# Blocks of 3, 2 and 3 matmul pairs, transposed maxima evicted by ScalarE in the first gap, and maxima 12 steps ahead

## The reference

```
for c in range(6):                      # 6 nodes, each on 4 sequences
    q = ew[c,0] * (nodes[in_q] @ We[eq] + be[eq])    # k and v alike
    scores = (q @ Wq[c]) . (k @ Wk[c]) / sqrt(16)    # 8 heads, 1024 x 1024
    attn = softmax(scores)
    nodes[c] = act_w[c] * (attn @ (v @ Wv[c])) @ Wo[c] + q
out = layernorm(nodes[5])
```

## Time and profile before

| | |
|---|---|
| median of 3 runs | 2479.15 us (2472.24 to 2482.92) |
| profiled execution: its time | 2468.93 us |
| its span in the trace | 2467.0 us |
| PE busy | 2297.7 us, 93% |
| DVE busy | 2062.4 us, 84% |
| ACT busy | 1787.8 us, 72% |
| POOL busy | 466.2 us, 19% |

### The profile page before, as it was taken

One profiled execution on the slowest core, in us unless ns is written; L12 is line 12 of the kernel. 1 busy time (PEld: TensorE's weight loads), 2 busy tenths in 40 slices (PEclk: granted clock), 3 DMA queues, 4 the chain that ended last, 5 costly groups with the idle time before them and its releaser, 6 DMA issues.

```text
span 2467.0 us, 40455 instructions
## 1 busy us (share of the span) xinstructions
PE 2297.7 (93%) x15067; PEld 929.7 (38%) x15067; DVE 2062.4 (84%) x2319; ACT 1787.8 (72%) x3425; POOL 466.2 (19%) x594
## 2 busy tenths in 40 slices
PE   6588899999999999999999999999999999999996
PEld 3433333333333333333433333333433333433332
DVE  6477778888888888888889888888888888889883
ACT  3225566777777777778777777778778778787775
POOL 1311121121121121121121121121121122123201
PEclk8568998999999999999999999999999999999998
DMA  3311131341342332332332242242232242242201
GB/s 95 79 31 32 27 60 40 63 83 46 73 76 50 71 73 53 68 73 54 68 73 55 66 75 51 52 76 50 51 77 49 52 77 53 47 86 58 60 16 49
DMA packets 75938, 147.43 MB, mean 60 GB/s; under 512 B 21451, under 2 KB 39135, under 8 KB 75743
## 3 DMA queue, kind: packets, MB, share of 16 engines
q0 software_dynamic: 28800, 96.49, 21.1%
q1 hardware_dynamic: 46942, 48.36, 7.3%
HBM read 40.40 MB, written 13.34 MB: 22 GB/s over the span
## 4 chain that ended last, share of the span: by engine, by line
PE 78%; DVE 13%; ACT 5%; issue 2%; POOL 1%; DMA 1%; SPq 0%; POOLq 0%; ACTq 0%; DVEq 0%
PE ring L431 29%; PE context L483 28%; DVE max_neg L979 8%; PE wide L453 7%; ACT e_ring L730 5%; PE ring L381 2%; PE ring L401 2%; PE ring L373 2%; PE ring L392 2%; PE ring L406 2%; DVE max_part L983 1%; PE ring L304 1%; PE ring L462 1%; PE ring L305 1%; DVE mixing L778 1%
## 5 line engine op out<-in xcount | busy, mean ns | idle before, releaser
L979 DVE TENSOR_REDUCE max_neg<-wide 128x1 f32<-128x1024 f32 x1536 | 1825.8, 1219 | 301.6 <-PE wide L453 289.4
L730 ACT ACTIVATE e_ring<-ring 128x512 f32<-128x512 f32 x3072 | 1628.6, 603 | 438.8 <-PE ring L431 437.2
L453 PE MATMUL wide<-k_aug,q_aug 48*128 48x512 f32 x3072 | 1128.2, 454 | 67.6 <-DVE max_neg L979 52.7
L431 PE MATMUL ring<-q_aug,k_aug 50*128 50x512 f32 x3072 | 1095.2, 446 | 4.8 <-ACT e_ring L730 3.1
L483 PE MATMUL context<-e_ring,v_aug 128*32 128x512 f32 (+1 forms) x7696 | 870.7, 525 | 0.1
L431 PEld LDWEIGHTS ring<-q_aug,k_aug 50*128 50x128 f32 x3072 | 502.3, 186 | 814.7 <-ACT e_ring L730 510.6
L453 PEld LDWEIGHTS wide<-k_aug,q_aug 48*128 48x128 f32 x3072 | 499.1, 188 | 152.2 <-DVE max_neg L979 117.2
L483 PEld LDWEIGHTS context<-e_ring,v_aug 128*32 128x32 f32 x7696 | 152.0, 108 | 280.7 <-issue 224.3
L263 POOL DMA_DIRECT2D src<-node_dram x40 | 23.7, 593 | 719.8 <-PE ring L392 719.8
L1056 POOL CAST q_part<-q_part 128x512 fp32r<-128x512 f32 x48 | 29.4, 612 | 445.2 <-ACT q_part L659 444.9
L1056 POOL CAST k_part<-k_part 128x512 fp32r<-128x512 f32 x48 | 29.3, 611 | 341.3 <-ACT k_part L651 341.2
(11 more groups left out here) (230 smaller groups left out, 876.4 us busy)
## 6 DMA issues: line engine op xcount, KB each, us to landing
k_aug<-k_part POOLq DMA_DIRECT2D x144, 256.0 KB, 7.1
q_aug<-q_part POOLq DMA_DIRECT2D x144, 256.0 KB, 7.3
src<-node_dram POOLq DMA_DIRECT2D x40, 512.0 KB, 5.5
ctxT<-raw SPq DMA_DIRECT2D x384, 32.0 KB, 2.0
rden_bc<-rden_dram SPq DMA_DIRECT2D x23, 512.0 KB
node_dram<-node_ring SPq DMA_DIRECT2D x16, 512.0 KB, 2.9
q_aug<-max_rows SPq DMA_DIRECT2D x384, 4.0 KB
node_ring<-in_L_attn_x SPq DMA_DIRECT2D x4, 512.0 KB, 5.1
```

What stands on the lines that cost most here:

```text
L431: e.matmul(bk[:, :], k_aug[first:first + AUG, u % 2, h // 2, chunk * P:(chunk + 1) * P].bitcast(F32R), q_aug[first:first + AUG, u % 2, h / ...
L453: done = e.matmul(wide[w % 2][:, half_of(kh)], q_aug[first:first + SPLIT, u % 2, h // 2, q0:q0 + P].bitcast(F32R), k_aug[first:first + SPL ...
L730: e.activation(e_ring[:, n % E_SLOTS, :], bank[where["st", n]][:, :], ACT.Exp, scale=EXP_SCALE).then_inc(a_exp, 1)
L979: e.tensor_reduce(max_neg[:, G % 2, row:row + 1], wide[w % 2][:, :], AX_X, ALU.max, negate=True).then_inc(v_mx, 1)
```

## The change

- The blocks are 3, 2 and 3 pairs: pairs 0, 1, 2, first gap, pairs 3, 4, second gap, pairs 5, 6, 7, third gap. What the second gap holds (a half of `weighted`, or the product) stays. So w2, pairs 4 and 5, now has the second gap between its two matmuls, and the product takes the ring bank after pair 4.
- ScalarE evicts a product after the first tile of the odd step (pair 4) and no longer after the second; `evict_v` on VectorE moves from behind w2 to behind w1.
- `turn_maxima` moves from the second gap to the end of the first, and ScalarE (between its exponentials of pairs 2 and 3) does `evict_rows` in place of VectorE. `move_max` follows in the same step; before, the copy came one step and the move two steps after the transposition.
- LOOKAHEAD is 12 and no longer 14. Groups finish at the same distance, so the split and the transposition stand at r = 4, 12, 20, 28 (before r = 2, 10, 18, 26).
- The late parts of the mixing layer start at steps -12, 6, 24, 42 (before -14, 5, 23, 42).
- `normalise` stands in GpSimd's program at r = 12, second half, before at r = 11, first half.

```
-LOOKAHEAD = 14
+LOOKAHEAD = 12
...
-        LATE_AT = ((4, -14), (5, 5), (6, 23), (7, 42))
+        LATE_AT = ((4, -12), (5, 6), (6, 24), (7, 42))
...
+        def finished(s):
+
+            G, rest = divmod(s + LOOKAHEAD, NCH)
+            return [G - 1] if rest == 0 and 0 < G <= GROUPS else []
...
+                for G in finished(s):
+                    turn_maxima(G, next_bank())
                 pairs(s, (3,))
-                pairs(s + 1, (0, 1))
-                G = (s + LOOKAHEAD - 1) // NCH
-                if s % NCH == 2 and 0 <= G < GROUPS:
-                    turn_maxima(G, next_bank())
+                pairs(s + 1, (0,))
                 if product:
                     product()
                 elif before:
                     weighted(s - 1, half_of_bank(1), False, True)
-                pairs(s + 1, (2, 3))
+                pairs(s + 1, (1, 2, 3))
...
+            def evict_rows(G):
+                if G >= 2:
+                    e.wait_ge(d_max_in[G % 2], DMA * HG * (G // 2))
+                e.wait_ge(p_turn, G + 1)
+                e.activation(max_rows[:, G % 2, :], bank[where["max", G]][0:2 * NR, 0:P], ACT.Copy).then_inc(a_neg, 1)
...
-                    if k == 1:
+                    if k == 0:
                         stages(s)
+                    if k == 2:
+                        for G in finished(s):
+                            evict_rows(G)
...
-                    if half == 0 and r in V_AT:
-                        evict_v(nxt, V_AT.index(r))
+                    if half == 1 and r + 1 in V_AT:
+                        evict_v(nxt, V_AT.index(r + 1))
...
-                    if half == 0 and r == 11:
+                    if half == 1 and r == 12:
                         normalise(prev)
...
+                if half == 1:
+                    for G in finished(s):
+                        move_max(G)
                 if half == 0:
-                    G = (s + LOOKAHEAD - 3) // NCH
-                    if s % NCH == 4 and 0 <= G < GROUPS:
-                        move_max(G)
```

More of the change, by code:

```diff
@@ L129, in build @@
             "a_td a_wt a_we a_be a_fold a_xT a_ek a_er a_r1 a_node")
-        a_exp, a_k1, a_q1, a_oa, a_cv, a_ft = sems("a_exp a_k1 a_q1 a_oa a_cv a_ft")
+        a_exp, a_neg, a_k1, a_q1, a_oa, a_cv, a_ft = sems("a_exp a_neg a_k1 a_q1 a_oa a_cv a_ft")
         v_own, v_omm, v_order, v_var, v_y, v_pad, v_ekv, v_den, v_prod, v_inv, v_gate, v_x2, v_var2, v_n2 = sems(
             "v_own v_omm v_order v_var v_y v_pad v_ekv v_den v_prod v_inv v_gate v_x2 v_var2 v_n2")
-        v_mx, v_cmb, v_neg, v_v, v_rec, v_fvar, v_fn, v_ctx, v_lvar, v_z, v_bo = sems(
-            "v_mx v_cmb v_neg v_v v_rec v_fvar v_fn v_ctx v_lvar v_z v_bo")
+        v_mx, v_cmb, v_v, v_rec, v_fvar, v_fn, v_ctx, v_lvar, v_z, v_bo = sems(
+            "v_mx v_cmb v_v v_rec v_fvar v_fn v_ctx v_lvar v_z v_bo")
         g_own, g_half, g_ident, g_vones, g_kones, g_rs1, g_rs2, g_rsf, g_rsl, g_r1, g_gate = sems(
@@ L463, in turn_maxima @@
                             ident[:, :]).then_inc(p_turn, 1)
-                freed[at] = (v_neg, G + 1)
+                freed[at] = (a_neg, G + 1)
             def weighted(z, columns, first, last):
@@ L1007, in vector_program @@
                     stages(s, half)
-                    G = (s + LOOKAHEAD - 2) // NCH
-                    if half == 0 and s % NCH == 3 and 0 <= G < GROUPS:
-                        evict_rows(G)
                 if s % 2:
@@ L1185, in move_max @@
                 r = G % 2
-                e.wait_ge(v_neg, G + 1)
+                e.wait_ge(a_neg, G + 1)
                 if u >= 2 and g == 0:
```

## The result

The changed kernel takes 2547.93 us (median of 4 runs, 2545.29 to 2550.86) against 2480.33 (now 4 runs): ratio 1.0279, 95% interval 1.0251 to 1.0306. It is 2.8% slower. The forecast was 2544, in a range of 2478 to 2564.

The account below looks back on a forecast made before the run. It took a loop through w2's and w3's reductions and pair 2 as the bound: 94.47 against 91.40 us a unit, 21 x 3.07 = 64.5, plus 3 and 1.9, less 4.3, +65 on 2479.15: 2544, range 2478 to 2564.

Parts of the forecast that it names:

- loop of part 1: Pair 5, reductions of w2 and w3, pair 2 (2.97), back to pair 5: iterations without product 5.20 us, before 4.97.
- wait in front of pair 2: PE waits for w3's tensor before pair 2's wide matmul in most iterations, some 0.5 us each.
- old blocks: Before the change, pair 7 to pair 2: 1.73 us against PE's 1.89, with PE waiting only behind a v copy.
- Iterations after a k or q product: Iterations such as r = 2 and 10, following k or q products: 5.20 us each, pair 7's wait lying inside 2.97.
- Part 3: Split at r = 4 and 12: at r = 12 `normalise` makes the cast 0.24 us late, pair 4 too: +0.32.
- Part 4: Inversion of the sums (0.54 us) behind w3's reduction at r = 5, hidden before: +0.53 at r = 6.
- Part 2: Transposition in the first gap: +0.22 or 0.23 us, four times a unit; ScalarE's copy of the rows costed at nothing.
- The ends: First two units +3 us (0 to 6.1), last unit +1.9, 12 steps ahead in place of 14: -4.3.
- ScalarE's copy at 4 x 0.3 a unit: Cost of the row copy on ScalarE if uncovered, in front of the exponentials of pairs 3 to 7; costed at nothing.
- loop's own range: 2518 to 2564 us, for the case that the loop decides (2544, 72%).
- faster rival: PE's own way decides, w2 and w3 being reduced when the third gap ends: -2.3 us a unit, 2427; 15%.

Follow-up runs that it names:

- e1: Changed kernel with the blocks of before (3, 3, 2 pairs; product and its eviction back in their old places): 2464.45 us, ratio 0.9975 to the kernel before.
- e4: Changed kernel with w2's reduction over half of its columns: 2447.38 us, ratio 0.9904 to the kernel before.
- e5: Kernel before with w2's reduction over half of its columns: 2447.23 us, ratio 0.9889 to the kernel before.
- e7: Changed kernel with blocks of 3, 2, 3 only in iterations without a product, 3, 3, 2 in the others: 2520.64 us, ratio 1.0187 to the kernel before.
- e8: e1 with GpSimd's `normalise` waiting until the split of r = 12 is done: 2448.21 us, ratio 0.9904 to the kernel before.
- e9: Changed kernel with the copy of the transposed rows on VectorE again: 2559.26 us, ratio 1.0374 to the kernel before.
- e10: e8 with the copy of the transposed rows on VectorE: 2448.42 us, ratio 0.9916 to the kernel before.

## Why the prediction was right, point by point

- **The loop of part 1** held, and it was nearly the whole loss (3.64 of 3.77). From one pair 2's wide matmul to the next the changed kernel takes 6.12 to 6.16 for k and q (6.14), 6.98 for the output (6.99), 6.36 for v (6.30), 6.34 with the transposition at r = 4 (6.36). e1 shows where the loss lies, e4 against e5 by which tile, e7 that it goes by way of pair 2.
- **The wait in front of pair 2** was forecast at some 0.5 in most iterations. It is there in 14 of 16, but 0.13 to 0.45 long, 0.23 on the mean of all. 0.45 comes at r = 4, 8 and 12, behind iterations without product. Elsewhere a part of the same 0.5 is spent earlier on PE's way: at r = 4 pair 7 comes 0.52 after pair 6 (1389.20 to 1389.72) in place of 0.23, as it waits for the product's eviction, and the gap behind it is longer for that. The length of the loop was right, the place of the wait was not.
- **The old blocks** were read too well. The prediction has w3's reduction wait for pair 7 alone (1.73 against PE's 1.89) and PE wait for it only behind a v copy. Without a product VectorE reaches w3 only when w2 is done, and by the earlier trace rows it ends 0.03 too late; e5 shows 1.07 a unit of such latenesses. The sum does not use them, as the lengths before were read from the trace.
- **Iterations after a k or q product** were mis-sized, the largest miss in the unit. From pair 2 to pair 2 they take 5.48 and 5.49 (r = 2, 10) for 5.20. Pair 7's wait for the product's eviction was taken as lying inside the 2.97. It does, but it makes pair 7 itself a late pair, so the third gap costs 1.42 (1389.72 to 1391.14) and pair 2 is on time. Then the wait of pair 4 for w0's reduction, which lay hidden behind a late pair 2, comes to light. The changed kernel at r = 10 (start 1402.94):

```profile
1403.51 0.46 PE L458 MATMUL wide<-k_aug,q_aug 48*128 48x512 f32 x1
...
1403.75 2.53 DVE L992 TENSOR_REDUCE max_neg<-wide 128x1 f32<-128x1024 f32 x2 [0.32 <-PE wide L458]
...
1404.82 0.40 PE L436 MATMUL ring<-q_aug,k_aug 50*128 50x512 f32 x1
1405.03 0.49 PE L458 MATMUL wide<-k_aug,q_aug 48*128 48x512 f32 x1
...
1406.02 0.50 PE L436 MATMUL ring<-q_aug,k_aug 50*128 50x512 f32 x1
```

  Pair 2 is at 0.57, the first reduction ends at 1403.75 + 1.22 = 1404.97, and pair 4's wide matmul comes at 1405.03, 0.21 behind its score matmul. That and the late gap behind it are the 0.3. Together r = 2 and 10 are 0.57 above the forecast, r = 18, 20 and 28 0.37, the v products 0.12; r = 6 and 12 are 0.32 below. This is 3.77 for 3.07, within 0.04.
- **Part 3** held in kind and not in size: the collision moved from r = 2 and 10 to r = 12, but cost the cast 0.11 for 0.24. In e1, where w3 is not late, the cast is held up by 1.15 (1.32 for 0.17), and e8 shows what that costs, 0.89 in the iteration and 0.78 in the unit. The 0.24 was also too small by its own rows: the cast ends 0.04 behind GpSimd's instruction, which makes it 0.28. The rule cited from the Trainium skill ("SBUF — State Buffer", section "Who interferes with whom") thus mattered more than its 0.32 in the sum: it is the difference between e1, equal to before, and e8, 1% faster.
- **Part 4**, the inversion at r = 6, was forecast at 0.53 and cost about 0.16 (5.19 against 5.03 at r = 2 and 10). It follows a k iteration too, where w3 is early, so most of the inversion stayed hidden: w0's reduction starts 1.02 into the iteration where it starts at 0.80 in r = 10.
- **Part 2**, the copy at no cost: right (0.27 on ScalarE, e9, e10).
- **The ends** were off, in parts that cancel: the first score starts at 147.0 and not at 163.5, 12 more than the 4.5 forecast, and the first two units take 14.5 more for 3. What in them is the mixing work passing the border and what the clock (0.62 for 0.58 between 106 and 147 us in the profiled executions) was not separated.

In the sum 3.07 a unit was forecast and 3.77 came, 15 us over 21 units. One more unit is 4 us longer for a stretch of 10 us with a granted clock of 0.67, part of it at 1.2 GHz. The profiled execution is thus 82 above that of before, while the medians are 68 apart. Part of the nearness of 2544 to 2548 is luck of that kind.

Two other sums of the prediction don't come out. ScalarE's copy at 4 x 0.3 a unit is 25 us over 21 units, so with the 3 of the first units the loop's own range would reach 2572 and not 2564. And the faster rival gives the iterations with a product their present lengths; by its prices one with k would be 2.46 + 1.32 + 0.34 + 0.34 + 1.06 = 5.52 and not 5.8, so that rival's time was put too high. Neither bears on the verdict.

## What to carry to other kernels

With two buffers between a producer that works in order and a slower consumer, don't ask how full the consumer is, but how long the way is from the tile that completes last to the tile that needs its buffer back, on both engines; cutting a tile by a gap brings two tiles together and makes that way longer. Price a change of order by closing that way into a loop: where no other way is longer, its length is the period, whatever the busy shares say. And look one iteration on for the lateness, since the iteration that causes it may itself be short.

## What the runs showed of the hardware

A VectorE cast of 128 x 16 values takes 0.17 us alone and 1.32 when it begins 1.11 into a GpSimd multiplication of 2.39, ending 0.04 after it each time (1360.32 after 1360.28; 1409.26 after 1409.22). The same copy of 32 x 128 values out of PSUM takes 0.27 us on ScalarE and on VectorE. A pair that had to wait makes the switch to other work behind it 0.1 us longer; that was counted from the earlier trace rows for pair 2, and came for pairs 4 and 7 as well.
